# Two stages of a Trainium2 kernel in one block, their edges written into each other

## What is computed

```python
# layer 0, per sample; v is x, q the condition, adj the integer edges
self_feat = concat(v, q or 0) @ W_self.T + b_self
for d in range(2):                       # edges and transposed edges, first 20 nodes
    aff = heads(self_feat @ Wq[d].T) . heads(kv @ Wk[d].T) / 4   # kv: first 20 rows
    aff = where(edge count > 0, aff, NEG) + label_bias
    output += per-head mix of kv by softmax(aff), times Wout[d], + bout[d]
x = v + relu(self_feat + output)
# layer 1; six modulation vectors come from silu(cond) @ ada_w.T
x1 = layernorm(x) * (scale1 + 1) + shift1
q, k, v = heads(x1 @ mat_qkv_w.T + bias);  q, k to unit length, q times a scale per head
x = x + (softmax(q k^T) v @ proj_w.T + proj_b) * gamma1
x = x + (gelu(x2 @ fc1) @ fc2 + b) * gamma2      # x2: like x1, of the new x
```

## Time and profile before

| what | us |
|---|---|
| median of 3 runs (lowest, highest) | 883.65 (879.73, 885.13) |
| the profiled execution, whole | 884.65 |
| its span, first to last instruction | 882.9 |
| PE busy | 780.6 |
| DVE busy | 497.3 |
| ACT busy | 482.4 |
| POOL busy | 372.4 |

### The profile page before, as it was taken

How to read it: one execution, slowest core, us unless ns; L and a number is a source line. 1 busy time by engine, 2 the same in 40 slices (tenths; PEclk the granted TensorE clock), 3 DMA queues, 4 the chain that set the end, 5 groups by cost and what they waited for, 6 DMA issues and landing times. The chain is left out here.

```text
span 882.9 us, 15507 instructions
## 1 busy us (share of the span) xinstructions
PE 780.6 (88%) x4964; PEld 570.7 (65%) x4964; DVE 497.3 (56%) x1018; ACT 482.4 (55%) x773; POOL 372.4 (42%) x622
## 2 busy tenths in 40 slices
PE   5989999999973459999999999999874899999997
PEld 3878788887851234655665666656542688888886
DVE  1278888888875345666666556555313544444432
ACT  1334444544440236777777777777662655555553
POOL 0157667666664364555555555554200222112210
PEclk9989999999995679999999999999987899999999
DMA  8601221212100067666666777776710000000001
GB/s 258 207 22 50 84 84 50 88 47 86 56 13 0 15 105 121 108 110 114 113 109 110 116 113 113 112 113 113 121 23 0 1 22 15 24 25 25 13 25 48
DMA packets 68460, 65.57 MB, mean 74 GB/s; under 512 B 10688, under 2 KB 67648, under 8 KB 68416
## 3 DMA queue, kind: packets, MB, share of 16 engines
q1 hardware_dynamic: 67088, 64.86, 36.0%
q10 hardware_dynamic: 1328, 0.16, 0.1%
HBM read 48.09 MB, written 16.78 MB: 73 GB/s over the span
## 5 line engine op out<-in xcount | busy, mean ns | idle before, releaser
L935 ACT ACTIVATE probsT<-ps 128x1024 f32<-128x1024 f32 x128 | 130.8, 1022 | 49.1 <-PE ps L1175 49.0
L1433 DVE TENSOR_TENSOR hidden_low<-hidden,hidden_high 128x512 fp32r<-128x512 f32 x64 | 46.1, 720 | 102.8 <-ACT hidden_high L1379 102.8
L1039 DVE TENSOR_REDUCE neg_max<-ps 128x4 bf16<-128x344 f32 x128 | 64.2, 512 | 60.1 <-PE ps L1143 59.2
L1175 PE MATMUL ps<-q_stack,k_stack 97*128 97x256 bf16 x512 | 80.0, 280 | 11.9 <-ACT probsT L935 5.7
L1175 PEld LDWEIGHTS ps<-q_stack,k_stack 97*128 97x128 bf16 x512 | 43.2, 99 | 69.5 <-issue 31.0
L1376 ACT ACTIVATE hidden<-ps,b_fc 128x512 f32<-128x512 f32 x64 | 44.2, 690 | 71.5 <-PE ps L1509 71.5
L1187 PE MATMUL ps<-probsT,v_ones 128*32 128x256 f32 x1024 | 69.4, 389 | 9.2 <-ACT probsT L935 9.1
L393 POOL TENSOR_TENSOR scores<-scores,row_max 128x640 f32<-128x640 f32 x32 | 40.7, 1272 | 79.1 <-DVE row_max L480 79.1
L1122 PE MATMUL ps<-w_qkv,x1T 128*128 128x512 f32 x128 | 67.7, 657 | 2.6 <-DVE rest L1046 1.5
L610 PE MATMUL ps<-x_res,w_q 128*128 (+1 forms) x256 | 65.6, 402 | 0.0
L1327 POOL TENSOR_TENSOR var_eps_f<-mean_var_f,ln_eps 128x4 f32<-128x4 f32 x8 | 2.4, 305 | 140.8 <-DVE mean_var_f L1405 140.8
(11 more groups left out here) (167 smaller groups left out, 1847.5 us busy)
## 6 DMA issues: line engine op xcount, KB each, us to landing
parts_dram<-parts SPq DMA_DIRECT2D x96, 128.0 KB
q_stack<-parts_dram SPq DMA_DIRECT2D x96, 128.0 KB, 4.4
adj<-in_adj SPq DMA_DIRECT2D x16, 440.0 KB, 4.2
k_stack<-parts_dram SPq DMA_DIRECT2D x16, 384.0 KB, 8.2
xT<-in_xT SPq DMA_DIRECT2D x16, 256.0 KB, 3.0
x_in<-in_x SPq DMA_DIRECT2D x16, 256.0 KB, 2.6
k_stack<-parts_dram SPq DMA_DIRECT2D x16, 256.0 KB, 9.0
out_x<-result SPq DMA_DIRECT2D x16, 256.0 KB, 2.1
```

The costliest lines, as they stand in the source:

```text
L935: nc.scalar.activation(probsT[:, s % 4, :], ps[:, 6:8, :].rearrange("p a n -> p (a n)"), ACT.Exp).then_inc(exp_made, 1)
L1039: nc.vector.tensor_reduce(places[:, :, k], ps[:, 3 + n % 2, 0:4 * KP].rearrange("p (a g) -> p a g", a=4), AX_X, ALU.max, negate=True).then ...
L1175: mm = nc.tensor.matmul(ps[:, 6 + j, kt * N:(kt + 1) * N], k_stack[:, par, place, kt * P:(kt + 1) * P], q_stack[:, par, place, :], start=T ...
L1433: nc.vector.tensor_tensor(hidden_parts[1][:, s % SLOTS, :], hidden[:, s % RAW, :], hidden_parts[0][:, s % SLOTS, :], ALU.subtract).then_in ...
```

## The change

- Graph and attention become one block, `graph_and_attention`. The graph's functions are taken over as they were, with new names where both stages had one (`outT` is `mixT`, DVE's `raw_scores` is `graph_scores`).
- The graph's last two turns (scores of sample 15, weights and mix of 14 and 15) and attention's prelude and turn 0 are written out by hand in one order for each engine. Statistics and normalising of sample 0 are in the graph turn before them (f = 15). The norm of sample 1, which stood in attention turn 0, is in that order too.
- PSUM banks of attention: q and k in banks 2 and 3 (before 0 and 1), the value product in 0 (before 2), the row maxima in 4 and 1 (before 3 and 4). The first transposes of `x_hat` go to bank 3. `turns` gets a first and a last turn.
- Buffers that turn 0 needs lie at the top. `parts` takes the place of `w_ada`, `qkn` shares `squares`. The stacks, `key_blocks`, `v_ones` and others lie over graph buffers, so they are written only after the graph's last residual (`x_made` at B).
- The constants `three_halves` and `row_head` are made in the set-up. POOL fills the half of `v_ones` that holds ones after `roots(0)`. The row of ones of `k_stack` comes by one transfer on SP's queue.

```diff
-def turns(turn, eng, stages):
+def turns(turn, eng, stages, first=0, last=B):
...
-    for i in range(5):
+    for i in range(first, 5):
...
-    for i in range(B - 1, B + stages - 1):
+    for i in range(B - 1, last):
...
+        parts = w_ada[:].rearrange("p k n -> p (k n)").bitcast(BF16).rearrange("p (a w s n) -> p a w s n", a=2, w=2, s=3)
...
+    qkn = squares
...
+    QK_BANK, PV_BANK, SIDE, COLS = 2, 0, 5, 6
+    ROW_BANKS = (4, 1)
+    MAX_BANK = ROW_BANKS[1]
...
+        sp.wait_ge(x_made, B - 2)
+        sp.dma_start(x_in[:, 1], t["x"][(B - 1) * N:B * N, :].rearrange("(t p) f -> p t f", p=P)).then_inc(x_arrived[1], 16)
+        put_part(0, 0, 0, high_made)
+        put_part(0, 0, 1, mid_made)
+        sp.wait_ge(x_made, B)
+        sp.dma_start(k_stack[KROWS:KROWS + 1].rearrange("o a h n -> o (a h n)").rearrange("o (p e) -> o p e", p=P),
+                     ones_b[:]).then_inc(key_ones_in, 16)
+        turns(turn, sp, 4, first=1, last=B + 3)
...
+            if isinstance(f, int) and f == B - 1:
+                norm_root(pool, nc, 0, mean_var, g, var_eps, rstd, mv_made, eps_made, rstd_made)
...
-        nc.gpsimd.memset(v_ones[:], 1.0).then_inc(ones_set, 1)
-        pool.wait_ge(ones_set, 1)
-        nc.gpsimd.memset(k_stack[KROWS:KROWS + 1], 1.0).then_inc(ones_set, 1)
...
+        shift(B - 1, 1, 0)
+        norm_root(pool, nc, 1, mean_var, g, var_eps, rstd, mv_made, eps_made, rstd_made)
+        shift(B - 1, 1, 1)
+        normalise(B - 1, 1, 0)
+        normalise(B - 1, 1, 1)
+        roots(0)
+        pool.wait_ge(x_made, B)
+        nc.gpsimd.memset(v_ones[:, :, :, :, HD:2 * HD], 1.0).then_inc(ones_set, 1)
+        blocks_of_pairs(0, 0)
+        low_part(0, 0, 0)
+        low_part(0, 0, 1)
+        turns(turn, pool, 4, first=1, last=B + 3)
...
         def square(f, tt):
             act.wait_ge(qk_out, T * f + tt + 1)
-            ge(act, ss_made, T * f)
+            ge(act, qkt_mm, 2 * f)
...
+        act.wait_ge(ada_out, 6 * C2)
+        shift_scale(0, 0, QK_BANK + 1)
+        take_weights(B - 2, 0)
+        exponentials(B - 1, 1, 0)
+        take_weights(B - 2, 1)
+        square(0, 0)
+        exponentials(B - 1, 1, 1)
+        take_values(B - 1, 1)
+        square(0, 1)
+        take_weights(B - 1, 0)
+        shift_scale(1, 1)
+        take_weights(B - 1, 1)
+        high(0, 0)
+        mid(0, 0)
+        turns(turn, act, 4, first=1, last=B + 3)
...
+            if isinstance(f, int) and f == B - 1:
+                moments(0)
...
+            if isinstance(f, int) and f == B - 1:
+                normalise(0)
...
+        graph_scores(B - 1, 1, 0)
+        moments(1)
+        graph_scores(B - 1, 1, 1)
+        take_qk(0, 0)
+        sums(B - 1, 1, 0)
+        take_qk(0, 1)
+        sum_squares(0, 0)
+        sums(B - 1, 1, 1)
+        sum_squares(0, 1)
+        first_guess(0)
+        normalise(1)
+        take_output(B - 2)
+        graph_residual(B - 2, 0)
+        unit_qk(0)
+        take_output(B - 1)
+        graph_residual(B - 1, 1)
+        dve.wait_ge(x_made, B)
+        dve.wait_ge(g["late_weights"], g["LATE"])
+        for k in range(C2):
+            nc.vector.tensor_scalar(b_gated[:, k, :], ada[:, k, :], b_proj[:, k:k + 1], None, ALU.mult).then_inc(gated_bias, 1)
+        rests(0, 0)
+        turns(turn, dve, 4, first=1, last=B + 3)
...
+        raw_scores(B - 1, 1, 0)
+        pe.wait_ge(q_out, 2 * C2 * B)
+        norm_transposed(0, QK_BANK + 1)
+        weights_of(B - 2, 0, 0)
+        pe.wait_ge(x_made, B - 2)
+        raw_scores(B - 1, 1, 1)
+        pe.wait_ge(g["late_weights"], g["LATE"])
+        make_qk(0, 0, 0)
+        values_transposed(B - 1, 0)
+        weights_of(B - 2, 0, 1)
+        pe.wait_ge(vt_mm, 2 * B - 1)
+        make_qk(0, 0, 1)
+        values_transposed(B - 1, 1)
+        graph_channels(B - 2, 0, B)
+        weights_of(B - 1, 1, 0)
+        graph_tokens(B - 2, B)
+        pe.wait_ge(aff_out, 2 * T * B)
+        norm_transposed(1)
+        weights_of(B - 1, 1, 1)
+        graph_channels(B - 1, 1, B)
+        graph_tokens(B - 1, B)
+        split_qk(0, None)
+        turns(turn, pe, 4, first=1, last=B + 3)
```

More of the change, by code:

```diff
@@ new lines, in roots, with low_part @@
+        def roots(f):
+            pool.wait_ge(seeded, 4 * (f + 1))
+            ge(pool, qkn_made, f)
+            for n in range(3):
+                newton(f, n)
+            by = root[0][:].rearrange("p (t w h) -> p t w h", t=T, w=2)
+            nc.gpsimd.tensor_tensor(by[:, :, 0, :], by[:, :, 0, :], head_scale[:].unsqueeze(1).broadcast_to([P, T, H]),
+                                    ALU.mult).then_inc(root_step, 1)
+        def low_part(f, par, w):
+            pool.wait_ge(mid_made, 2 * f + w + 1)
+            nc.gpsimd.tensor_tensor(parts[:, par, w, 2, :], rest[:, w, :], parts[:, par, w, 1, :], ALU.subtract).then_inc(low_made, 1)
@@ new lines, in turn @@
+        def turn(f, b, c, d, par):
+            ahead = following(f)
+            if ahead is not None:
+                norm_root(pool, nc, ahead, mean_var, g, var_eps, rstd, mv_made, eps_made, rstd_made)
+            if f is not None:
+                roots(f)
+                blocks_of_pairs(f, par)
+                low_part(f, par, 0)
+                low_part(f, par, 1)
+        shift(B - 1, 1, 0)
+        norm_root(pool, nc, 1, mean_var, g, var_eps, rstd, mv_made, eps_made, rstd_made)
+        shift(B - 1, 1, 1)
@@ L465, in turn, with shift_scale @@
                 take_queries(f, par, 1)
-        turns(turn, act, 3)
+        turns(graph_turn, act, 3)
+        def shift_scale(n, par, bank=SIDE):
+            act.wait_ge(xt_mm, n + 1)
+            ge(act, v_mm, n - 1)
+            for k in range(C2):
+                nc.scalar.activation(x1T[:, par, k, :], halves(ps, bank)[:, k, :], ACT.Identity,
+                                     bias=ada[:, 4 * C2 + k, bass.ds(n, 1)],
+                                     scale=ada[:, 2 * C2 + k, bass.ds(n, 1)]).then_inc(x1_out, 1)
@@ new lines, in high, with mid @@
+        def high(f, par):
+            ge(act, parts_out, 6 * 16 * (f - 1))
+            ge(act, s_mm, GROUPS * (f - 1))
+            for w in range(2):
+                act.wait_ge(qkt_mm, 2 * f + w + 1)
+                nc.scalar.activation(parts[:, par, w, 0, :], ps[:, QK_BANK + 1 - w, :], ACT.Copy).then_inc(high_made, 1)
+        def mid(f, par):
+            for w in range(2):
+                act.wait_ge(rest_made, 2 * f + w + 1)
+                nc.scalar.activation(parts[:, par, w, 1, :], rest[:, w, :], ACT.Copy).then_inc(mid_made, 1)
@@ new lines, in residual, with turn @@
+        def residual(d):
+            dve.wait_ge(res_mm, d + 1)
+            x = x_res[:, bass.ds(d * T, T), :].rearrange("p t f -> p (t f)")
+            nc.vector.tensor_tensor(x, ps[:, SIDE, :], x, ALU.add).then_inc(res_made, 1)
+        def turn(f, b, c, d, par):
+            ahead = following(f)
+            for s in range(SLOTS):
+                for n in groups(b, s):
+                    maxima(b, n)
+                if ahead is not None and s == 0:
+                    norm_stats(nc, x_res, ahead, stats, stats_made)
+                    dve.wait_ge(stats_made, T * (f + 2))
+                if f is not None and s == 1:
+                    sum_squares(f, 0)
+                if f is not None and s < 2:
+                    take_qk(f, s)
+                if ahead is not None and s == 0:
+                    norm_moments(nc, stats, mean_var, mv_made)
+                if ahead is not None and s == 2:
+                    normalise(ahead)
+                if f is not None and s == 2:
+                    sum_squares(f, 1)
+                    first_guess(f)
+                if d is not None and s == 3:
+                    divide(d)
+                if f is not None and s == 5:
+                    unit_qk(f)
+                if f is not None and s == 6:
+                    rests(f, par)
+                if d is not None and s == 8:
+                    residual(d)
@@ L1110, in norm_transposed @@
+                graph_tokens(c, B if b is None else b + 1)
+        turns(graph_turn, pe, 3)
+        def norm_transposed(n, bank=SIDE):
             pe.wait_ge(xhat_made, T * (n + 1))
```

749 lines of the change are left out of this document (335 added, 414 removed).

## The result

The changed kernel takes 855.25 us (median of 4 runs, 852.98 to 858.64) and the kernel before 884.39 us in the same comparison. The ratio is 0.9676, 95% interval 0.9617 to 0.9734, which is 28.7 us less. I forecast 857.9 us, 25.8 us less. The profiled execution took 852.98 us with a span of 851.0.

The account below looks back on a forecast made before the run. An edge emptied by handing one sample between engines was taken as what to shorten, PE setting the stages' pace. `split_qk(0)` at 277.8 in place of 303.6 saves 25.8: 883.65 - 25.8 = 857.9 us; 855 to 862 (0.62), overall 850 to 867.

Parts of the forecast that it names:

- the edge: Passage from graph to attention, about 264 to 330 us: nearly empty because one sample passes from engine to engine.
- The fills: POOL's fills of `v_ones` and `k_stack` hold up DVE's `x_hat` of sample 0; moving only them would gain 8.4 us.
- The chain by hand: New order followed from DVE's row maximum end in graph turn 15 (246.86) to `split_qk(0)`, at 275.6 us with full clock.
- PE's row of work: PE from the first `x_hat` transposes through both `make_qk` halves, without a gap: 8.3 us, to 262.9.
- DVE's row: DVE behind the second half of q and k, from `take_qk` through `normalise(1)`: 4.7 us, to 267.7.
- The clock term: Half clock for the last 5 us before `split_qk(0)`, moving its start from 275.6 to 277.8: 2.2 us.
- the rival of the early fall: Clock falls in PE's idle time before 254.6; PE's 8.3 us grow by about 7; 865.3 us, chance 0.14.
- my sum: `split_qk(0)` at 277.8 in place of 303.6 us, 25.8 less; taken from 883.65 this gives 857.9 us.
- The rival of the held clock: Clock stays up; `split_qk(0)` at 275.6, itself and turn 1's `make_qk` faster; up to 31 us, 852.6, chance 0.14.
- The lock of the ports: DVE's two `x_hat` instructions wait while POOL holds the shared ports: 0 to 2.5 us, taken as 1.1.
- Waits costed at nothing: Behind `split_qk(0)`: half fill 0 (0.9 uncovered), row transfer 0 (up to 2), `rests(0)`, PSUM banks and set-up 0.
- slower case: PE's clock stays low longer behind the edge; three attention turns at half clock would give 918 us; chance 0.05.

Follow-up runs that it names:

- the kernel with the low parts first: Changed kernel with both `low_part` of sample 0 ahead of its `blocks_of_pairs` on POOL; the time didn't move, first `col_scores` 23.50 us behind `split_qk(0)` against 25.20.
- the kernel with the fills on POOL: Changed kernel with POOL again filling all of `v_ones` and the `k_stack` row, behind the last graph residual, in place of half fill and transfer; 863.43 us.
- PE kept busy: Changed kernel with 16 transposes of the identity on PE before the first `x_hat` transposes; stretch to `split_qk(0)` 0.3 us shorter, total time not given.
- the early norm: Changed kernel with statistics, root and normalising of sample 0 in graph turn 4 in place of 15; stretch to `split_qk(0)` 26.90 us, the time didn't fall.
- the control: The kernel before, unchanged, run again under another name to show what a comparison resolves; last row maximum ended at 244.57 us against 246.86, total time not given.
- both short: Changed kernel with sample 0's norm in graph turn 4 and sample 15's weights and mix ahead of sample 1's norm; five runs between 851.13 and 851.98 us.
- the new order alone: Changed kernel with sample 15's weights and mix ahead of sample 1's norm, sample 0's norm still in graph turn 15; 851.65 us (850.36 to 852.63).

## Why the prediction held, and where it didn't

**What bounded the edge** was read rightly. The fills were 8.4 us, measured as 8.4 in PE's wait. The rest of the sum had 17.1 us for the interleaving. It measured 19.3 us in the stretch and 16 to 17 in the times. The barrier (0.34 us) was too small to show apart.

**The chain by hand.** Counted from the end of the row maximum, the prediction had these steps at 2.4 GHz, against the changed kernel: `x_hat` ready 7.6, measured 7.0; end of `normalise(1)` 20.8, measured 21.0; end of sample 1's transposes 23.0, measured 22.9; start of the mix of 15 25.1, measured 24.9; `split_qk(0)` 28.7, measured 28.8. The last agreement is luck. The count was for full clock, and the measured stretch has 1.7 us of half clock in it (next paragraph), so the same work at full clock takes about 27.0 us. The count was 1.7 us too long.

About half of that is PE's row of work. In the kernel with the low parts first, where it ran at full clock, it took 7.5 us (254.41 to 261.91) and not 8.3: each group of matmuls starts up to 0.2 us before the recorded end of the one ahead, and I had added whole durations. Another 0.6 us is `x_hat`, which was ready sooner. DVE's row went the other way, with 5.05 us for my 4.7, and my own terms (4.24 less 0.9 plus 1.2) add up to only 4.5.

**The clock term** of 2.2 us came out near its size, but in another place. I had put it on the last 5 us. The mix ran at full clock (1.95 us), and the fall came at about 272, for 0.4 us in `graph_tokens(15)`. Instead, the clock fell at about 251.2, in the hole that I had named for the rival of the early fall. That rival gave 7 us for PE's row of work. It cost 1.3, because the clock was back at about 254.6, before `make_qk` began. The price depends on when it comes back. In the kernel with the fills on POOL, the same program up to here, `make_qk` was caught too (2.56 us for its first half in place of 1.88), and PE's row of work ended 2.8 us later than at full clock. The three executions of these same instructions, 27.46, 28.78 and 31.93 us, show that such a term can only be a range. The 28.7 to 30.9 of my sum is too narrow at both ends.

**The rival of the held clock** counted up to 3 us behind the edge. `make_qk` of turn 1 did run at full clock (1.96 us for its first half). What that is worth shows from `split_qk(0)` to `split_qk(1)`, in kernels that are one program there. The rows are the start of `split_qk(1)` with PE kept busy, in the changed kernel and with the early norm:

```profile
290.22 1.97 PE L1206 MATMUL ps<-ident,squares 128*128 128x128 f32 x8 [3.95 <-DVE squares L944]
```

```profile
291.70 1.97 PE L1206 MATMUL ps<-ident,squares 128*128 128x128 f32 x8 [4.21 <-DVE squares L944]
```

```profile
294.19 1.97 PE L1206 MATMUL ps<-ident,squares 128*128 128x128 f32 x8 [4.19 <-DVE squares L944]
```

With PE kept busy all of `split_qk(0)` and `make_qk` ran at full clock, and it took 17.61 us. In the changed kernel `split_qk(0)` ran at half clock, and it took 18.40. With the early norm the clock was down to about 283, and it took 19.24. So the clock there is worth up to 1.6 us, about half of the 3 that the rival counted, since POOL's roots lie in the same chain. The kernel before took 18.64 us in its profile and 19.46 in the control's. The rival's condition wasn't met: the clock fell again at about 289, and its mean from 288 to 303 is 0.54.

**The lock of the ports.** I had 1.85 us for the two `x_hat` instructions, and they took 1.75, beside 0.82 in all when POOL is free. POOL's `normalise` (1.27 us each) ran meanwhile. The first of `first_guess`'s small instructions took 0.82 us in place of 0.20, and it ended as another of POOL's `normalise` ended (264.26). The cost that the Trainium skill (SBUF — State Buffer, "SBUF: two separate sides") puts on a busy POOL was there, 0.9 and 0.6 us, each below the length of the POOL instruction that ran.

**Waits costed at nothing.** The half fill was hidden, by 0.68 us. The transfer was hidden: it landed 2.8 us after its issue at 277.88, and no wait of turn 1 ended with it. The last graph residual came 2.5 us later in the count from the row maximum, below the 3 to 5 expected. `unit_qk` was done at 271.27, 2 us before PE came to it, as forecast (2.3). Banks and the shared buffer were nothing, as forecast.

**No slower case.** Attention's steady turn stayed at 21.1 us, and the low clock got shorter, not longer.

The measured saving is 2.9 us larger than forecast. Of that, 2.2 us lie in the stretch: 1.7 from the count, which was too long, and 0.5 from the clock. The rest is less than the kernel's own spread.

## What to carry to other kernels

Where one sample is handed from engine to engine at the edge of two stages, add up the steps of each of the two chains. If most engines are idle in both, write the end of the one into the start of the other. The most that this can gain is the length of the shorter chain. Here the graph's end took 27.2 us and attention's start, without the fills, 20.8; written into each other they took 28.8. Before that, look for constants being filled on POOL while DVE works. Here they cost 8.4 us, and one transfer and a half fill in a better place did the same for nothing. And a step moved out of the edge into a full turn can cost there as much as it saved, so measure that turn too.

## What the runs showed that I had not expected

The same program reached the end of its graph turns 2.3 us apart in two executions, and ran one stretch of some 28 us in 27.5 to 31.9 us. Both go with the granted clock. From 30 to 45 us it was 0.86 in the kernel before and 0.93 in the control and the changed kernel. Whole times go with it too: the four runs of the changed kernel took 852.98, 854.73, 855.76 and 858.64 us at mean clocks of 0.968, 0.961, 0.961 and 0.957.

The clock didn't answer to the holes alone. PE's hole before the `x_hat` transposes was 2.65 us in the changed kernel, in the one with the low parts first and in the one with the fills on POOL. With the low parts first the clock stayed at 1.00 through it. With the fills on POOL it fell in it, at about 250.4:

```profile
250.00:252.00 2.00, 0.86 (x4) 0.89 (x5) 2.00 (x5) 0.00 (x0) 0.52 (x1) 0.60 0.00 0
```

The second hole was 2.65 us in all of these too. In the three kernels in which the first hole was filled or short, the clock fell at the second. Of the three with both holes open, one had a fall at the first, one at both and one at neither. With both short it held through the stretch, in the one execution profiled. That kernel's times also had the narrowest spread, 0.9 us over five runs, where the kernel before has 7.5 over its 23 in the same comparison. But five runs are few, and the new order alone, with its first hole still open, has 2.3 over six. What decides whether a hole brings a fall stays open.

No kernel here kept the clock past turn 1. In the one with both holes short it was 0.51 from 282 to 298 us, where PE worked 7.41 of 16 us.
